# x turned inside the weight fold, lora A loads in groups, and VectorE's order in the attention units

## What is computed

```python
x = x + attn(cond(x, ids1, W1, b1, A1, B1), wq, wk, wv, wo)   # cond: x @ W1.T + b1 + 2 * (x @ A1[id]) @ B1[id]
                                                              # attn: rope, 32 q heads, 8 kv heads, causal softmax
x = x + ffn(cond2(x, ids2, W2, Wr2, A2, B2), Wf, bf, Af, Bf, Rf)   # gated LoRA experts, top 2 of 8 and of 16
```

## Time and profile before

| | us |
|---|---|
| median of 3 runs | 2788.17 |
| lowest and highest run | 2786.31, 2791.28 |
| the profiled execution, whole | 2785.69 |
| its span in the trace | 2783.7 |
| TensorE busy | 2691.8 (97%) |
| VectorE busy | 1362.2 (49%) |
| GpSimd busy | 1181.8 (42%) |
| ScalarE busy | 856.5 (31%) |
| mean granted TensorE clock | 0.992 |

### The profile page before, as it was taken

How to read it: one execution, slowest core, us unless ns; L and a number is a source line. 1 busy time by engine, 2 the same in 40 slices (tenths; PEclk the granted TensorE clock), 3 DMA queues, 4 the chain that set the end, 5 groups by cost and what they waited for, 6 DMA issues and landing times.

```text
span 2783.7 us, 37581 instructions
## 1 busy us (share of the span) xinstructions
PE 2691.8 (97%) x14520; PEld 2173.4 (78%) x14520; DVE 1362.2 (49%) x2019; ACT 856.5 (31%) x2089; POOL 1181.8 (42%) x782
## 2 busy tenths in 40 slices
PE   8889999999999999999999999999999999999999
PEld 7767777777777788887877777777777778888877
DVE  3123777777777111124533567777777711112552
ACT  2122344444444312211212334444444421121110
POOL 0015666555565244510303476555556433451020
PEclk9999999999999999999999999999999999999999
DMA  6854122222225333111544312222122543311322
GB/s 220 214 162 130 54 69 69 74 71 68 70 69 197 129 114 106 46 46 46 148 122 104 119 46 77 76 77 72 60 75 69 174 136 106 114 46 38 91 85 68
DMA packets 312498, 268.48 MB, mean 96 GB/s; under 512 B 68730, under 2 KB 283898, under 8 KB 312322
## 3 DMA queue, kind: packets, MB, share of 16 engines
q1 hardware_dynamic: 250722, 210.50, 24.9%
q10 hardware_dynamic: 61600, 55.58, 6.0%
HBM read 201.88 MB, written 64.16 MB: 96 GB/s over the span
## 4 chain that ended last, share of the span: by engine, by line
PE 86%; POOL 5%; ACT 3%; DMA 2%; issue 1%; SPq 1%; DVE 1%; ACTq 0%; POOLq 0%
PE prod L672 26%; PE prod L674 25%; PE prod L673 25%; PE turned L915 3%; PE turned L865 2%; POOL s_lo L1490 1%; ACT probs L1248 1%; PE turned L666 1%; POOL o_lo L1525 1%; ACT s_hi L1216 1%; PE turned L898 1%; PE prod L1101 1%; POOL w_lo L1455 1%; POOL w_sum L1515 1%; DMA raw<-in_wo 1%
## 5 line engine op out<-in xcount | busy, mean ns | idle before, releaser
L1455 POOL TENSOR_TENSOR w_lo<-raw,w_hi 128x1024 fp32r<-128x1024 f32 x96 | 236.1, 2461 | 838.5 <-ACT w_hi L1161 838.3
L672 PE MATMUL prod<-o_hi,w_hi 128*128 128x512 f32 x1024 | 402.8, 393 | 12.0 <-POOL o_lo L1525 8.5
L674 PE MATMUL prod<-o_hi,w_lo 128*128 128x512 f32 x1024 | 399.2, 390 | 0.0
L673 PE MATMUL prod<-o_lo,w_hi 128*128 128x512 f32 x1024 | 399.2, 390 | 0.0
L1814 DVE TENSOR_TENSOR x<-prod,x 128x512 f32<-128x512 f32 x128 | 88.5, 691 | 559.5 <-PE prod L674 559.5
L1490 POOL TENSOR_TENSOR s_lo<-w_sum,s_hi 128x512 fp32r<-128x512 f32 x192 | 251.2, 1308 | 243.5 <-ACT s_hi L1216 243.5
L1161 ACT CAST w_hi<-raw 128x1024 fp32r<-128x1024 f32 x130 | 136.1, 1049 | 620.9 <-PE prod L674 447.9
L672 PE MATMUL prod<-t_hi,s_hi 128*128 128x512 f32 x768 | 315.1, 410 | 10.5 <-POOL s_lo L1490 10.5
L674 PE MATMUL prod<-t_hi,s_lo 128*128 128x512 f32 x768 | 303.0, 394 | 0.0
L673 PE MATMUL prod<-t_lo,s_hi 128*128 128x512 f32 x768 | 302.6, 394 | 0.0
L1216 ACT CAST s_hi<-w_sum 128x512 fp32r<-128x512 f32 x192 | 118.9, 621 | 391.7 <-PE prod L674 216.4
(11 more groups left out here) (168 smaller groups left out, 5073.2 us busy)
## 6 DMA issues: line engine op xcount, KB each, us to landing
raw_pair<-in_wq SPq DMA_DIRECT2D x64, 512.0 KB, 3.7
o_scratch<-o_out ACTq DMA_DIRECT2D x64, 512.0 KB, 2.9
raw<-in_wo SPq DMA_DIRECT2D x64, 512.0 KB, 4.0
o_raw<-o_scratch SPq DMA_DIRECT2D x64, 512.0 KB, 6.9
raw<-t_scratch SPq DMA_DIRECT2D x50, 512.0 KB, 3.6
t_scratch<-x ACTq DMA_DIRECT2D x17, 512.0 KB, 4.6
x_raw<-in_x SPq DMA_DIRECT2D x16, 512.0 KB, 6.1
xt_scratch<-x_sum SPq DMA_DIRECT2D x16, 512.0 KB, 3.2
```

Of the source, the lines that this page charges most:

```text
L672: pe.matmul(dst, wh, xh, start=start, stop=False)
L673: pe.matmul(dst, wh, xl, start=False, stop=False)
L674: return pe.matmul(dst, wl, xh, start=False, stop=stop)
L1455: pool.tensor_tensor(WL[i % 2][:], RAW[i % 2][:], WH[i % 2][:].bitcast(F32), ALU.subtract).then_inc(w_lo, 1)
```

## The change

1. SyncE issues the 16 loads of lora A in four groups of four, ahead of the W2 tiles of steps 5, 6, 7 and of B2 (step 8), instead of all ahead of tile 6.
2. TensorE turns the first four blocks of x inside fold steps 7 and 8. From TW block 12 on, TW blocks use bank TP[0] alone and these blocks of x bank TP[1] alone. ScalarE's casts and VectorE's remainders of x move into the fold too.
3. At the start of each half TensorE does c_main(1) before it waits for a_lo and does h_lora(0). ScalarE casts W1 tiles 2 and 3 as soon as c_main(0) and c_main(1) are done (a new semaphore, first_used).
4. In late units and in q2/q3 units VectorE adds and rotates the first head before the mask of the even set, and normalises the even set before the mask of the odd set.

```diff
-                if i == 6:
+                if i >= 5:
                     sp.wait_ge(const_in, 16 * 5)
                     sp.wait_ge(fold_taken, 4)
-                    load_a1(0)
+                    load_a1(0, 4 * (i - 5), 4 * (i - 5) + 4)
...
+        def tw_bank(n):
+            return TP[n % 2 if n < 12 else 0]
+        def x_bank(hf, b):
+            return TP[1 if hf == 0 and b < 4 else b % 2]
...
             def turn_tw(n):
                 pe.wait_ge(tw_in[n % 4], tw_round(n))
-                if n >= 2:
+                if n >= 13:
+                    pe.wait_ge(tw_copied, n)
+                elif n >= 2:
                     pe.wait_ge(tw_copied, n - 1)
-                turn_block(n % 2, TW_IN[n % 4], P, tw_turned)
+                turn_block(tw_bank(n), TW_IN[n % 4], P, tw_turned)
+            def turn_x(hf, b):
+                pe.wait_ge(x_in[b], 16 * (hf + 1))
+                if hf == 0 and b == 0:
+                    pe.wait_ge(tw_copied, 12)
+                elif hf == 0 and b < 4:
+                    pe.wait_ge(xt_lo, b)
+                elif hf * TB + b >= 2:
+                    pe.wait_ge(xt_lo, hf * TB + b - 1)
+                turn_block(x_bank(hf, b), XR[b], P, turned)
...
+                        elif i == KC - 1 and k == KC - 2 or i == KC and k == (KC - 2, 2)[t]:
+                            turn_x(0, 2 * (i - KC + 1) + t)
...
                 c_main(0, chunk=first_chunk)
+                c_main(1)
                 pe.wait_ge(a_lo, hf + 1)
                 hold(pe)
                 h_lora(0)
-                c_main(1)
...
-                tile_hi(hf, 2, QN["h0"])
+                for n in range(2):
+                    act.wait_ge(first_used, 2 * hf + n + 1)
+                    tile_hi(hf, n + 2)
...
+                        dve.wait_ge(p1_in, n + 1)
+                        add_head(A_C11, PR_2, X0[:], 0, 0, 0)
                         if late:
                             mask(4 * (gg - 1) + 2)
                         if qd == QD_23:
                             mask(4 * gg)
-                        dve.wait_ge(p1_in, n + 1)
-                        add_head(A_C11, PR_2, X0[:], 0, 0, 0)
                         add(A_U2, X0[:], PR_6, X0[:])
                         dve.wait_ge(quad_in, quad_at(n, A_U2))
                         add(A_U3, XU[:], PR_7, X0[:])
                         if late:
+                            normalise(4 * (gg - 1) + 2)
                             mask(4 * (gg - 1) + 3)
-                            normalise(4 * (gg - 1) + 2)
                         if qd == QD_23:
+                            normalise(4 * gg)
                             mask(4 * gg + 1)
-                            normalise(4 * gg)
```

More of the change, by code:

```diff
@@ L272, in build @@
         taken = sem("taken")
+        first_used = sem("first_used")
         cb_hi = sem("cb_hi")
@@ L453, in adapter, with load_a1 @@
                                      min_val=0, max_val=SLOTS - 1)
-            def load_a1(hf):
-                for n in range(TT * SPT):
+            def load_a1(hf, lo=0, hi=TT * SPT):
+                for n in range(lo, hi):
                     t, n8 = n // SPT, n % SPT
@@ L661, in _, with turn_block @@
             pe.wait_ge(ident_in, 16)
-            def turn_block(par, raw, rows, done):
+            def turn_block(bank, raw, rows, done):
                 for c in range(KC):
-                    mm = pe.transpose(TP[par][:, c * P:c * P + rows], raw[0:rows, c * P:(c + 1) * P],
+                    mm = pe.transpose(bank[:, c * P:c * P + rows], raw[0:rows, c * P:(c + 1) * P],
                                       ident[0:rows, 0:rows])
@@ L695, in _ @@
             hold(pe)
-            turn_block(0, ER, M_AR, fold_turned)
+            turn_block(TP[0], ER, M_AR, fold_turned)
             def turn_wf(b):
@@ L701, in turn_wf @@
                     pe.wait_ge(fold_split, b)
-                turn_block((b + 1) % 2, X1[:, b * D:(b + 1) * D], P, fold_turned)
+                turn_block(TP[(b + 1) % 2], X1[:, b * D:(b + 1) * D], P, fold_turned)
             def fold_bank(q):
@@ L745, in _ @@
             hold(pe)
[L747 to L754, removed]
             for hf in range(HALVES):
@@ L775, in c_main @@
                     bank_free(q)
-                    main(q, n % 2, tiled(XTH[t]), tiled(XTL[t]), stop=False, chunk=chunk)
+                    mm = main(q, n % 2, tiled(XTH[t]), tiled(XTL[t]), stop=False, chunk=chunk)
+                    if n < 2:
+                        mm.then_inc(first_used, 1)
                 def c_lora(n):
@@ L1131, in tw_copy, with x_hi @@
                     act.wait_ge(tw_stored[n % 4], tw_round(n - 4))
-                act.copy(TW_OUT[n % 4], TP[n % 2][:]).then_inc(tw_copied, 1)
+                act.copy(TW_OUT[n % 4], tw_bank(n)[:]).then_inc(tw_copied, 1)
                 act.wait_ge(tw_copied, n + 1)
                 act.dma_start(t_d[n], TW_OUT[n % 4]).then_inc(tw_stored[n % 4], 16)
+            def x_hi(hf, b):
+                t, c = b // BPT, (b % BPT) * P
+                act.wait_ge(turned, hf * TB + b + 1)
+                act.copy(view(XTH[t][:], KC, c, c + P), view(x_bank(hf, b)[:], KC)).then_inc(xt_hi, 1)
             for i in range(KC + 1):
-                if i >= 1:
-                    for n in range(2 * i - 2, 2 * i if i < KC else TW_N):
-                        tw_copy(n)
+                if 1 <= i < KC - 1:
+                    tw_copy(2 * i - 2)
+                    tw_copy(2 * i - 1)
+                elif i == KC - 1:
+                    tw_copy(12)
+                    x_hi(0, 0)
+                    tw_copy(13)
+                    x_hi(0, 1)
+                elif i == KC:
+                    tw_copy(14)
+                    x_hi(0, 2)
+                    x_hi(0, 3)
+                    tw_copy(15)
+                    tw_copy(16)
                 if i + 2 <= KC:
@@ L1149, in _ @@
             act.wait_ge(const_in, 16 * 5)
[L1151 to L1154, removed]
             def tile_hi(hf, i, free=None):
@@ L1161, in tile_hi @@
                 act.copy(WH[i % 2][:], RAW[i % 2][:]).then_inc(w_hi, 1)
-            for b in range(4):
-                x_hi(0, b)
             tile_hi(0, 0)
@@ L1187, in c_hi @@
                                    ).then_inc(cb_hi, 1)
-                tile_hi(hf, 2, QN["h0"])
+                for n in range(2):
+                    act.wait_ge(first_used, 2 * hf + n + 1)
+                    tile_hi(hf, n + 2)
                 c_hi(0)
-                for n in range(1, KC):
+                c_hi(1)
+                for n in range(2, KC):
                     c_hi(n)
@@ L1612, in _, with x_lo @@
             chain(0, dve.tensor_scalar(LB[:], LB[:], LANG_BIAS, None, ALU.mult))
+            def x_lo(hf, b):
+                t, c = b // BPT, (b % BPT) * P
+                dve.wait_ge(xt_hi, hf * TB + b + 1)
+                dve.tensor_tensor(view(XTL[t][:], KC, c, c + P), view(x_bank(hf, b)[:], KC),
+                                  view(XTH[t][:].bitcast(F32), KC, c, c + P), ALU.subtract).then_inc(xt_lo, 1)
             for i in range(1, KC + 1):
@@ L1618, in _ @@
                     take(i, n)
[L1620 to L1627, removed]
+                    if i >= KC - 1 and n < 2:
+                        x_lo(0, 2 * (i - KC + 1) + n)
             for hf in range(HALVES):
```

## The result

The changed kernel takes 2803.1 us (median of 9 runs, 2797.5 to 2813.0), the kernel before 2790.1 us (median of 9, 2786.3 to 2792.2). The ratio is 1.0054, with a 95% interval of 1.0044 to 1.0064: 12 to 18 us slower. The forecast was 2800. The time was right, but not every term of it: the front gave 20 us and not 24.5, and part 4 cost the 37 us of the forecast, but along two paths where I had seen one, and with 2.5 us of it in a place forecast as nothing.

What follows compares the result with a forecast made beforehand. TensorE, busy 97% of the span, was taken as the bound, so only its waits or clock matter. From 2785.7 us, 24.5 gained and 37 lost gave 2798; with runs' median 2.5 us higher, forecast 2800, range 2768 to 2812.

Steps and rivals of the forecast that it cites:

- the front: Parts 1 to 3 together, in the fold and at the start of both halves: 24.5 us gained.
- the shift: Late units: even exponentials, held up through GpSimd, delay the s_hi cast and L915 by 1.5 us, 14 times: 21 us lost.
- the q2/q3 units: Part 4's same swap in these units: even exponentials 1.9 us later with 3 us to spare, so nothing lost.
- the clock: Late units: 10 of 14 gaps of 3.3 us before L915 followed by half clock, 1.6 us each: 16 us lost.
- Lora A loads: Fold: groups of four loads end the late W2 tile of step 6 and its half clock: 12.6 us gained.
- x in the fold: Passage from fold to half 0: idle time goes, less turns, remaining waiting and a stall in step 7: 0.8 us gained.
- c_main(1) ahead: Start of both halves: the second W1 product covers the wait for lora_a_lo: 6.0 and 5.1 us gained.
- L880 buys nothing: Late units: ending the 1.35 us wait before the probabilities' transpose only lengthens the L915 wait, so pays nothing.
- B: Late units: even exponentials still end before the cast, only the front counts: 2764, up to 2780 us; chance 0.20.
- A: Late units: the shift without the clock, or half the shift with some of it: 2785 us, no difference; chance 0.24.
- C: Late units: the change does what it says, the 18.9 us at L880 are gained: 2745 us; chance 0.04.
- D: Fold gives less, B2 4.6 us later or step 5's tile late: up to 2808 us; chance 0.52 together with the forecast.

Runs made afterwards that it cites:

- e3_no_fold_x: The kernel before with parts 1 and 3 alone, x turned after the fold in two banks: 2767.3 us.
- e11_best: Parts 1 to 3, normalise ahead of the odd mask, probs_t ahead of the odd exponentials in late units, last two lora A groups behind B2: 2733.9 us.
- e9_head: Parts 1 to 3 plus only the first head's move ahead of the even set's mask, normalise left behind the odd mask: 2804.4 us.
- e5_norm_pout: Parts 1 to 3 with the even set normalised ahead of the odd mask, and ScalarE copying probs_t ahead of the odd exponentials in late units: 2741.4 us.
- e1_front: The changed kernel with VectorE's order of the kernel before, so parts 1 to 3 alone: 2768.4 us.
- e6_pout: Parts 1 to 3 with ScalarE copying the even set's probs_t ahead of the odd exponentials in late units, VectorE as before: 2762.2 us.
- e12_after_pout: The changed kernel, all four parts, with ScalarE copying the even set's probs_t ahead of the odd exponentials in late units: 2757.8 us.
- e4_norm: Parts 1 to 3 plus only the even set's normalising moved ahead of the odd set's mask, first head left behind the even mask: 2791.2 us.

## Why the prediction was right, and where it wasn't

The sum was 2785.7 - 24.5 + 37 = 2798; the execution whose trace is shown took 2803.1 (a span of 2801.2), and 2785.7 - 20 + 37 = 2803. The terms missed in both directions: the front by 4.5 us, the shift by 3 and the q2/q3 units by 2.5 made it slower, the clock by 5 made it faster. That so little is left of them is luck in part.

- **Lora A loads, 12.6 us.** Held for the W2 tiles: no W2 wait, and step 6 takes 14.51 us. But the last group also made B2 late, and that alone costs 3.6 us in e3_no_fold_x, without x in the fold; the forecast had put the whole price of it under x.
- **x in the fold, 0.8 us gained.** Failed: 4.9 us lost against before. The passage came as worked out (4.80 us of waiting at the new end, 4.8 forecast). The term that was mis-sized is the stall before TW block 13: 2.4 us with bounds 1 and 5, measured 5.59, and 2.5 us of half clock behind it that the sum left out. B2 was cast 5.9 us later than before (15.4 against 9.5 us after step 7's start), above the forecast's upper bound of 4.6. The step behind it priced four lora A loads at the mean of sixteen, 1.13 us each; they took 2.2 us each. The first product of half 0 came 6.9 us earlier and not 13.5; with the stall gone, in e11_best, it comes 14.1 us earlier.
- **c_main(1) ahead, 6.0 and 5.1 us.** Held: h_masked costs 0.94 us, twice, and the stretches up to the attention units are 7.4 and 5.2 us shorter. The first is over the forecast by its clock: two half-clock stretches of 6.8 us stood in the passage before (behind the 4.56 and the 4.63 us of the earlier trace rows), a single one of 3.4 us after.
- **Late units, 1.5 us each.** The size held (1.7), and so did the mechanism: the even exponentials at the head of the chain, late by the rotation step and neg_max that wait for GpSimd. What I missed is the score bank, a second path that is 1.0 us late on its own. It didn't change the sum, since the two run side by side. It did change its places: L931 waits 2.6 us and not 3.3, and the missing part stands before the scores. It also means that mending the exponentials alone could not have won the 1.5 back. The 0.2 us through GpSimd's s_lo were missing too.
- **The clock, 10 of 14.** It was 7 of 14 in this execution, at the 1.6 us forecast: 11 us and not 16. 14 x 1.7 + 11 + 2.5 (q2/q3) = 37: the sum was right partly because the last term, forecast as nothing, filled in. One reading behind the 10 was weak: the 1.80 us gap of the earlier trace rows didn't stand alone. A wait of 2.36 us had ended at 310.2, 4.6 us before that gap began, with half clock from 310.6 to 314.0 behind it.
- **L880 buys nothing.** Held, and more than held: with the normalise swap alone, which does remove that wait, the kernel is 23 us slower than without.
- **The rivals.** B (no shift) was ruled out by the 2.6 us at L931 and the 1.7 us from group to group. A (the shift, with few or no drops of the clock) wasn't far off: 7 of 14 gaps were followed by half clock in the execution shown, and only 3 of 14 in that of e9_head, which has the same waits. C, the change does what it says, needed the ScalarE edit of e5_norm_pout. D's late B2 came true, and beyond its 4.6 us.

## What to carry to other kernels

A wait is worth its length only if the next wait on the same engine doesn't grow by it: before moving work to end one, ask what the instruction behind it waits for, and move both or neither. Before an operation is moved back in its engine's list, list everything that waits for each of its steps, also those that only free a buffer. The issue time of a DMA in a crowded queue isn't a price that can be cut in pieces: sixteen loads took 18.15 us, four groups of four of them took 4.1, 4.5, 6.7 and 8.7.

## What the hardware showed

- **Joining two short gaps can cost more than either.** Waits of 1.35 and 0.43 us with a product of 3 us between them were never followed by half clock (0 of 14 in the kernel before and in e1_front), nor was a single 1.35 or 1.02 us (e6_pout, e12_after_pout). The two joined, in one piece of 2.2 us, were in 12 of 14 (e4_norm). But 2.6 us with another 1.04 us 10 us ahead of it was in only 7 of 14, and in 3 of 14 in e9_head, so the length of the gap doesn't decide by itself. What else does was not tried and stays open. The changed kernel's nine runs spread over 15 us, with a granted clock from 0.988 to 0.994, where the kernel before spreads over 6.
- **GpSimd and VectorE delay each other both ways.** VectorE's rotation step and neg_max ended 0.55 and 0.03 us after the GpSimd operation beside them, in the kernel before and in the changed one alike, though the GpSimd operations beside them were different ones; GpSimd's s_lo took 1.49 us beside VectorE's normalise and 1.29 us without. In each of these cases the delayed operation was the one that had started second.
